# An attention and mixture-of-experts kernel on one core: moving the last output-weight load and the first expert's down weights, and putting identity transposes into three of TensorE's waits

## The reference

```python
x = x + xattn(layernorm(x), ctx)      # both sides rounded to fp8 by blocks of 128, then one product
h = layernorm(x)
# ffn(h):
a = h + attention(rmsnorm(h)) @ o_w.T # 16 query heads, 4 key/value heads, rope, causal softmax
t = rmsnorm(a)
probs = softmax(t @ gate_w.T)         # 8 experts
topv, topi = top_k(probs, 2)          # weights topv / (sum(topv) + 1e-9)
moe = sum_e combine[e] * ((silu(t @ wg[e].T) * (t @ wu[e].T)) @ wd[e].T)   # I = 352
out = x + a + moe
```

## Time and profile before

| | |
|---|---|
| median of 3 runs | 1390.86 us (1388.47 to 1391.62) |
| the profiled execution | 1391.31 us |
| its span | 1389.5 us |
| PE busy | 1255.7 us, 90% of the span |
| DVE, ACT, POOL busy | 842.7, 715.9, 384.9 us |
| mean granted clock of PE | 0.966 of full speed |
| moved by the DMA engines | 228.5 MB, 164 GB/s in the mean |

### The profile page before, as it was taken

One profiled execution on the slowest core, in us unless ns is written; L12 is line 12 of the kernel. 1 busy time (PEld: TensorE's weight loads), 2 busy tenths in 40 slices (PEclk: granted clock), 3 DMA queues, 4 the chain that ended last, 5 costly groups with the idle time before them and its releaser, 6 DMA issues. The chain is left out here.

```text
span 1389.5 us, 22860 instructions
## 1 busy us (share of the span) xinstructions
PE 1255.7 (90%) x6845; PEld 1012.8 (73%) x6845; DVE 842.7 (61%) x2480; ACT 715.9 (52%) x2290; POOL 384.9 (28%) x545
## 2 busy tenths in 40 slices
PE   1777899999999999989999999999996499999995
PEld 0466667778776777777767777878775498899995
DVE  7678776767886786578768665666644422222221
ACT  6447665565674566476656646556543033333331
POOL 0223121214322132322223233332210124333331
PEclk9988999999999999999999999999998699999998
DMA  3270335432355466738445664855304788877433
GB/s 99 75 283 28 121 107 183 174 129 92 152 165 178 161 212 200 250 113 243 166 158 188 209 204 151 264 194 184 104 4 133 277 318 218 247 211 205 77 62 38
DMA packets 89894, 228.50 MB, mean 164 GB/s; under 512 B 12272, under 2 KB 50032, under 8 KB 79536
## 3 DMA queue, kind: packets, MB, share of 16 engines
q1 hardware_dynamic: 63712, 184.03, 37.7%
q0 software_dynamic: 10848, 24.71, 9.8%
q10 hardware_dynamic: 15216, 18.30, 3.7%
HBM read 146.76 MB, written 80.24 MB: 163 GB/s over the span
## 5 line engine op out<-in xcount | busy, mean ns | idle before, releaser
L537 POOL TENSOR_TENSOR prob<-prob,rtotal 128x128 f32<-128x128 f32 (+2 forms) x192 | 119.2, 626 | 405.3 <-DVE rtotal L1297 379.0
L960 ACT ACTIVATE prob<-prob,bias 128x128 f32<-128x128 f32 (+3 forms) x256 | 145.1, 567 | 155.1 <-DVE prob L1291 154.3
L1291 DVE TENSOR_SCALAR_CACHE_REDUCE prob<-bank,nscale 128x128 f32<-128x128 f32 (+3 forms) x256 | 134.9, 546 | 147.1 <-PE bank L716 146.8
L735 PE MATMUL bank<-pT,v 128*128 128x512 f32 (+3 forms) x512 | 175.8, 445 | 9.0 <-ACT pT L966 8.3
L680 PE MATMUL bank<-w_hi,hT_hi 128*128 128x512 f32 x480 | 173.4, 361 | 4.1 <-DVE rot L1256 4.0
L966 ACT ACTIVATE pT<-bank 128x512 f32<-128x512 f32 (+3 forms) x256 | 102.9, 432 | 130.0 <-PE bank L724 129.8
L680 PE MATMUL bank<-w_hi,hT_lo 128*128 128x512 f32 x480 | 162.2, 338 | 0.0
L680 PE MATMUL bank<-w_lo,hT_hi 128*128 128x512 f32 x480 | 162.0, 337 | 0.0
L1602 PE MATMUL gu<-we,xT_hi 128*128 x624 | 156.5, 332 | 3.2 <-DVE xT_lo L1718 2.7
L514 POOL TENSOR_TENSOR r<-r,rot 128x640 f32<-128x640 f32 x60 | 99.3, 1655 | 196.1 <-DVE rot L1256 196.1
L714 PE MATMUL bank<-kT_hi,qT_hi 128*128 128x128 f32 (+3 forms) x256 | 101.8, 397 | 20.8 <-DVE prob L1291 20.8
(11 more groups left out here) (312 smaller groups left out, 2852.9 us busy)
## 6 DMA issues: line engine op xcount, KB each, us to landing
w_hi<-ws_scratch SPq DMA_DIRECT2D x24, 1024.0 KB, 5.2
w_lo<-ws_scratch SPq DMA_DIRECT2D x24, 1024.0 KB, 7.8
we<-wx_scratch SPq DMA_DIRECT2D x16, 1408.0 KB
we<-wx_scratch SPq DMA_DIRECT2D x16, 768.0 KB, 10.9
stage<-in_wexp SPq DMA_DIRECT2D x64, 176.0 KB, 2.4
wx_scratch<-ehi ACTq DMA_DIRECT2D x64, 176.0 KB, 2.0
wx_scratch<-stage SPq DMA_DIRECT2D x64, 176.0 KB, 2.5
stage<-in_wqkvo SPq DMA_DIRECT2D x40, 256.0 KB, 3.6
```

The lines of the kernel that those rows point to most:

```text
L537: nc.gpsimd.tensor_tensor(p, p, rtotal[:, 4 * h + q:4 * h + q + 1].broadcast_to([P, KEYS[q]]), ALU.mult).then_inc(prob_ready, 1)
L735: nc.tensor.matmul(bank[PV][:, j * P:S], v[it % (LAG + 1)][:, j, :], pT[:, PT_AT[j]:PT_AT[j] + QS[j]], start=(j == 0), stop=(j == TT - 1)) ...
L960: nc.scalar.activation(p, p, ACT.Exp, bias=bias[:, 4 * h + q:4 * h + q + 1], scale=-1.0, accum_out=total[:, 4 * h + q:4 * h + q + 1]).then ...
L1291: nc.vector.tensor_scalar(prob[(G * it + h) % (LAG + 1)][:, P_AT[q]:P_AT[q] + KEYS[q]], bank[SC + q % 2][:, 0:KEYS[q]], nscale[it % 2][:, ...
```

## The change

1. **The last output weights.** Iteration 15's output weights go into chunks 0 to 3 of `w`, where the q weights lay, and are loaded in iteration 15 at place (0, 1) by a new `load_last_o`, once all q projections are done. `wo` and the wait in `output` follow.
2. **The order of SP's transfers in `moe`.** Expert 0's gate and up weights come right behind the tables. Its down weights wait for `extra_saved`, and the zero rows come behind them.
3. **The wait for `dispf`** moves from before the first `choose` to before its third instruction, the first one that reads the table.
4. **Identity transposes** (`keep_busy`, the identity turned into a PSUM bank that nobody reads then): 56 after `first_products`, 40 after the first projections, 50 before `transposes(0)` in `moe`.

```diff
-        def wo(i, h):
-            return w[i][:, QKV + h, :]
+        def wo(o, i, h):
+            return w[i][:, h if o == NIT - 1 else QKV + h, :]
...
+            def load_last_o():
+                sp.wait_ge(projq, TT * NIT)
+                for i in range(2):
+                    sp.wait_ge(o_saved[i], 16 * HKV)
+                    sp.dma_start(w[i][:, 0:KC, :].rearrange("p c n -> p (c n)").bitcast(F32), ws_dram[HKV - 1, i, :, QKV * CH:NCH * CH]).then_inc(wq_in[i], 16)
...
+                        if (it, h, place) == (NIT - 1, 0, 1):
+                            load_last_o()
...
-                if it >= HKV:
+                if HKV <= it < NIT - 1:
                     load_o(it)
...
+            def keep_busy(o, count):
+                for _ in range(count):
+                    nc.tensor.transpose(o, ident[:, :], ident[:, :])
...
-                            pe.wait_ge(wo_in[i], 16 * (o - HKV + 1))
+                            pe.wait_ge(*((wo_in[i], 16 * (o - HKV + 1)) if o < NIT - 1 else (wq_in[i], 16 * (NIT - HKV + 1))))
...
             first_products()
+            keep_busy(bank[PV][:, 0:P], 56)
             for t in range(TT):
                 transposes_h(0, t)
...
             for t in range(TT):
                 project(0, t, True)
+            keep_busy(bank[PV][:, 0:P], 40)
             for i in range(G):
                 transpose_qk(0, i)
...
             sp.dma_start(dispf[:, :], dispf_d).then_inc(f_in, 16)
             sp.dma_start(disph[:, :], disph_d).then_inc(h_in, 16)
+            load_expert(sp, 0, False)
+            sp.wait_ge(extra_saved, 32)
+            load_expert(sp, 0, True)
             sp.wait_ge(zeroed, 1)
             for n in range(3):
                 sp.dma_start(out[B * S + n * P:B * S + (n + 1) * P, :], zrow[:, :]).then_inc(pad_saved, 16)
-            load_expert(sp, 0, False)
-            load_expert(sp, 0, True)
             sp.wait_ge(pad_saved, 16 * 3)
...
             last.then_inc(inverted, 1)
+            keep_busy(dn[1][:, 0:P], 50)
             transposes(0)
...
                 own.chain(V.tensor_tensor(eq[:, :, :], values, wide(best[c]), ALU.is_equal))
+                if c == 0:
+                    dve.wait_ge(f_in, 32)
                 own.chain(V.tensor_tensor(eq[:, :, :], eq[:, :, :], order, ALU.mult))
...
-            dve.wait_ge(f_in, 32)
             choose(prob[:, :, :], 0, c1)
```

More of the change, by code:

```diff
@@ L751, in output @@
                     for n, (a, c) in enumerate(SPLITS):
-                        last = nc.tensor.matmul(bank[t % 2][:, :], aT[a][:, (G * o + h) % RING_A, t * P:(t + 1) * P], wo(c, h),
+                        last = nc.tensor.matmul(bank[t % 2][:, :], aT[a][:, (G * o + h) % RING_A, t * P:(t + 1) * P], wo(o, c, h),
                                                 start=(h == 0 and n == 0), stop=(h == G - 1 and n == 2))
```

## The result

The forecast was 1386.8 us, faster than before by 4.1 us. Measured on one chip, the changed kernel took **1392.55 us** (median of 20 runs, 1388.38 to 1397.07) and the kernel before 1390.33 us (20 runs, 1383.85 to 1393.03): **1.0019 times before, 95% interval 1.001 to 1.0027**. It is slower, by 2 to 3 us. A second comparison beside other kernels gave 1.0024 (1.0007 to 1.0041). The profiled execution took 1393.47 us, span 1391.7 us.

The account below looks back on a forecast made before the run. PE was busy 90% of the span, so time could go only where it idles or runs at the lower clock. Hand-over 3.2, start 0.9 and output weights 0 sum to 4.1 us: 1386.8 us, range 1383.0 to 1390.2.

Parts of the forecast that it names:

- Extra columns: Mixer-to-experts stretch: small transfer, 15.06 us before, lands at 1081.8 to 1086 with fewer weights beside it; gather 2.1 us earlier.
- Rival 1: Extra columns stay late, landing at 1092.0; the gather meets weights and zero rows, 5.5 us: 1388.8 us, chance 0.2.
- The table wait: Before the experts: wait moved behind two VectorE instructions, so all that follows on VectorE comes 0.65 us earlier.
- The failed step: First gather before the experts: may meet the last zero rows, costed at nothing, with 4 us of slack as cover.
- The second failed step: First expert tile: fillers raise the clock, so the first 24 gate and up products gain 1.9 us.
- the fillers, not the gather, would end last: Before the first tile: 50 fillers end at 1096.3, gathered rows land at 1094.95; transposes start 0.8 us earlier.
- The start: First 150 us: 56 and 40 fillers gain 0.2 at the first wait, 0.6 at the second, 0.1 behind: 0.9 us.
- Rival 3: Start, 92 to 98 us: the forty fillers keep the clock up, 1.7 us more won: 1385.1 us, chance 0.15.
- The last output weights: End of the mixer: loading them 44 us earlier gains nothing, bounds 0.2 us either way.
- hand-over: From mixer to experts, 1068 to 1100 us: 0.8 + 0.5 + 1.9 = 3.2 us won.
- 2: Before the first tile: the fifty fillers run at half clock, 11 us, transposes 2.6 us later: 1393.7 us, chance 0.09.
- Rival 4: Nothing reaches the end: the 3.2 us return as waits in the expert loop or start: 1390.5 us, chance 0.06.

Follow-up runs that it names:

- e1_order: Kernel before with only the new order of SP's transfers in moe and the moved table wait, no fillers: 1.0011 times before, 1390.21 us.
- f_nofront: Changed kernel without the start's 56 and 40 fillers: 1.0003 times before, 1390.91 us.
- g_zero_late: Changed kernel without the start's fillers, zero rows only after the first gather's landing, 35 instead of 50 fillers before the transposes: 0.9984 times before, 1387.48 us.
- h_after128: Changed kernel with 32 more fillers ahead of TensorE's first work, 128 in all before the mixer: 0.9999 times before, 1389.99 us.
- f_through: Kernel before with only 50 fillers ahead of the first real transposes and 16 behind them: 0.9985 times before, 1387.55 us.
- h_start128: Kernel before with only the start's 56 and 40 fillers and 32 more ahead of TensorE's first work: 1.0007 times before, 1390.00 us.
- h_best128: f_best with the start's 56 and 40 fillers and 32 more ahead of TensorE's first work: 0.9983 times before, 1387.37 us.
- f_best: Kernel before with reordered transfers, moved table wait, zero rows after the first gather, 35 and 16 fillers around the first transposes: 0.9987 times before, 1388.18 us.

## Why the prediction was wrong

**Extra columns: right.** Issue to landing went from 15.06 to 8.9 us. Counted from the tables' issue they landed at what would be 1086.1 on the clock of before, the late end of the forecast, and 5 us before VectorE's row numbers. Rival 1 fell. What they meet most of the way is no longer weights but POOL's add, which the forecast named only in passing. The packets of 1084 to 1086 us in the changed kernel, to be read beside the earlier trace rows:

```profile
q0 software_dynamic: 186, 0.38, 102.3%
q10 hardware_dynamic: 186, 0.00, 13.3%
q1 hardware_dynamic: 18, 0.02, 3.9%
```

186 to 186 is turn by turn again, a tiny packet of the columns for each one of the add. The Trainium skill (DMA: Bandwidth & Descriptors, Queues, rings and completion order) has the turn-taking between queues, with which this agrees; its 9 to 17 descriptors to a packet this trace doesn't show for 12-byte pieces, since the columns took 186 turns in these 2 us alone.

**The table wait: 0.65 us at best.** e1_order has its row numbers 0.65 us earlier (+21.49 against +22.14), the changed kernel's own profile 0.28, since its table took longer to land.

**The failed step: "The gathers, issued from 1091.4 on, may meet the last zero rows. I cost it at nothing."** That was the term to size. The cover I named, 4 us of slack of the gate weights' announcement, covered something else; the gather itself had none. And I had the price: in rival 1 I gave the same meeting "say 5.5 us", and in my own sum nothing. Beside the zero rows it takes 5.2 to 5.7 us where the trace has its last landing (two more traces have the first transposes 6.3 and 7.0 us behind its issue), and 3.5 us where they come later and the down weights stay in front of it. It was forecast to start 2.1 us sooner and did so by 1.7 us (2.0 in e1_order); all of that is given back. Taking this one overlap away brings the second tile 2.0 us forward (f_nofront to g_zero_late).

**The second failed step: "the first products 4.2 and not 6.14 us, 1.9 won".** They took 5.57 us. The estimate of the fillers was good: 50 took 7.75 us where 7.6 was forecast (6.6 to 7.7 in the other traces). But I had the clock follow from the fillers alone and forgot that between the four transposes and the products lies a wait of 1.7 to 2.8 us, for ScalarE's and VectorE's split. Of the six traces with fillers only ahead of the transposes the granted clock falls in that wait, or within 0.4 us of its end, in four, and in a fifth already in the wait for the gather; in the sixth, of h_after128, it stayed up, the products took 4.2 us, and the second tile came at +37.1. With 16 fillers in that wait it stayed up through the first tile in all three traces, though in f_through's it fell in the next one. That the fillers, not the gather, would end last was wrong too, for the first reason.

**The start: 0.9 us forecast, 0.46 us found.** The 0.6 us of the third query head is there as 0.46. The 0.2 us of the first place is nothing: VectorE's stretch behind it is unchanged.

**Rival 3 (the clock stays up through 98 us) is real, but the forty don't decide it.** From VectorE's 200th to its 250th instruction (93 to 113 us) four traces take 18.4 us, with the clock up all the way; the other thirteen, the changed kernel's two among them, take 19.9 to 20.7 us. That is 1.6 us, close to the 1.7 I gave. But of these four only h_start128 has fillers at the start; e1_order, f_nofront and f_through have none. The stretch in f_through, to be read beside 0.72 in the earlier trace rows and 0.80 in the changed kernel:

```profile
92.00:98.00 6.00, 4.42 (x25) 3.54 (x25) 5.36 (x18) 2.20 (x8) 0.97 (x2) 0.97 0.54 221
```

**The last output weights: nothing, right.** The output products are released as before, their first row has the same wait of 1.64 us as in the earlier trace rows.

```profile
1053.26 0.47 PE L764 MATMUL bank<-w_hi,aT_hi 128*128 128x512 f32 x1 [1.64 <-issue]
```

**What no step had.** Fillers that end within the wait they fill cost TensorE nothing there and still move all that is behind them in its stream. With 96 of them an instruction packet falls on a saving of rows, and 0.5 to 1.1 us go there.

**The sum in its place.** Forecast 4.1 us gained. Shown in the changed kernel's two traces: start +0.46 in both; saving of rows at 740 us, -0.7 and -1.1; hand-over -0.2 and -1.2 us. That makes a loss of 0.4 and 1.9 us, against 2.2 and 3.2 measured in medians. The rest stays open. Part of it may be chance: single executions differ by what the next section tells.

The rivals: 2 named slower and the right time (1393.7), but not by its mechanism, since by their mean price some 30 of the 50 fillers ran at 2.4 GHz. Rival 4 (nothing reaches the end) came nearest, through the gather and not through the expert loop. Its time should have been 1390.0 and not 1390.5 by its own terms (1386.8 and the 3.2 of the hand-over). The loop keeps a lead more often than not: h_best128 and h_after128 have 2.9 and 2.8 us at the second tile and still 2.7 and 2.5 at the end, while f_best's trace lost 2.0 of its 2.9 there.

## What to carry to other kernels

Before a transfer is moved out of the way of one small transfer, look at what is issued next in its new place: bulk that nobody waits for (here zero rows) belongs behind the landing of the last small transfer that somebody waits for. Fillers that keep TensorE's clock up must fill every wait up to the work they are for, the short ones behind the first real instruction too. And where a change adds instructions to an engine's stream, compare the traces stretch by stretch far from the edit, since what is shown for one place of the stream can move with their number.

## What was not expected of the hardware

- *Short stretches at the lower clock in the middle of busy work.* At 442, 562, 630, 814 and 1016 us a trace either has a short stretch at 1.2 GHz or has not, and each costs 1.0 to 1.7 us (up to 3 at 562 us, where it sometimes lasts twice as long). Between the same VectorE instructions (1000th to 1100th) all seventeen traces have 51.0 or 52.5 us, nothing between. The stretch at 1017 us, in the changed kernel and in before:

```profile
1017.00:1021.00 4.00, 3.80 (x8) 2.03 (x9) 0.46 (x3) 1.42 (x5) 1.29 (x2) 0.57 0.01 2
```

```profile
1017.00:1021.00 4.00, 4.00 (x21) 2.94 (x20) 1.19 (x5) 2.31 (x7) 0.83 (x1) 1.00 0.00 0
```

  The Trainium skill (TensorE: Matmul & The Clock Gate, Part 1) says the clock's watching of activity runs free of the kernel; that the same kernel has such a stretch in one trace and not in the other fits this: the changed kernel has one at 1017 us in its first trace and none there in its second. Why they come at these places no run shows. A trace has one to four of them, which can be a good part of the 9 us by which runs of one kernel differ.
- *A mean clock tells little here.* The changed kernel had 0.975 of full clock in its profile and before 0.966, and it was slower: the fillers raise the mean in stretches where nobody waits for TensorE.
- *An instruction packet on another engine's DMA issues:* up to 3.47 instead of 1.91 us for four issues on SP, in a place set by the number of TensorE's instructions. By the three kernels with 128 fillers this is reversible; how the one delays the other the traces don't tell.
